# Last stage of a two-layer transformer kernel: PE issue order changed, last normalise as one scaled pass on ACT, last residual sum on DVE

## The chip, the cores and the metric

The kernel runs on one core of a Trainium2 chip. A core has five engines that run apart and meet through semaphores: TensorE (PE, matmuls), VectorE (DVE), ScalarE (ACT), GpSimd (POOL) and SyncE (SP), which here only issues DMAs. The metric is the device time of one execution in microseconds, and lower is better.

## The reference, cut to what matters

1024 tokens of width 512 pass through four sublayers, and after each one the sum of its input and its output is normalised. The change touches the last sublayer and the two normalisations around it:

```python
def _layernorm(x, axis=-1, eps=1e-05):
    m = jnp.mean(x, axis=axis, keepdims=True)
    v = jnp.var(x, axis=axis, keepdims=True)
    return (x - m) / jnp.sqrt(v + eps)

    dots = jax.nn.softmax(x @ centroids.T / TEMPERATURE, axis=-1)
    hits = dots > THRESHOLD
    query_sel = jnp.any(hits, axis=1)
    cluster_sel = jnp.any(hits, axis=0)
    row_sel = cluster_sel[assignments]
    dense = x @ weight.T + bias
    out = jnp.where(query_sel[:, None] & row_sel[None, :], dense, jnp.zeros((), dense.dtype))

x = _layernorm(x + _L0_attn_ref(...), axis=-1)
x = _layernorm(x + _L0_ffn_ref(...), axis=-1)
x = _layernorm(x + _L1_attn_ref(...), axis=-1)
x = _layernorm(x + _L1_ffn_ref(...), axis=-1)
```

`cluster_sel` needs the hits of all 1024 tokens, so no output row can be finished before the softmax over the 64 clusters is done for every token. The centroid matrix has 64 clusters.

## The kernel before, in words

Each sublayer is a stage of its own. The change lies in `gqa_stage`, after its loop over the eight key heads, where the last head is finished and the last sublayer is computed. The order of the work on every engine there is written out by hand: each engine's block lists its instructions, and semaphores hold one back until another has finished. Nothing is reordered by a scheduler. The tokens are eight tiles of 128 (`TT` = 8, `ST` = 4, so four tiles make one half, `b` = 0 or 1). Every fp32 product is made of three terms, high by high, low by high and high by low, so a merge, a logits step and a dense tile have 12 matmuls of 512 columns in groups of four, and a dense tile has two more for the bias.

The helpers that the prediction speaks of are these.

- On PE, `merge(True, tk, j)` adds the attention output of tile j in PSUM (line 1840), `turn_x(t)` transposes the normalised tile t into `ps_s` (line 1922), `logits(b)` multiplies one half by the centroids (line 1930), `turn_logits(b)` transposes the logits (line 1939), and `dense_tile(t, begin, end)` does the matmuls begin to end of 14 of dense tile t (line 1953). Between them two small steps count the hits (line 1988) and spread the chosen columns over the partitions (line 1992).
- On DVE, `sum_out(t)` adds a merge to X and takes mean and variance (lines 1687, 1681, 1683), `norm(t, base)` takes the reciprocal of the deviation and normalises X (lines 1694, 1696), and `low_x(t)` makes the low part of the turned tile (line 1701). `shift_logits` and `take_hits` are the softmax and the hits of one half (lines 1715 to 1730). The last loop over t does one masking pass of a dense tile out of PSUM (line 1764), then mean and variance of tile t-1 (`finish`) and the normalise of tile t-2.
- On ACT, `root(t, base)` is the square root of the variance (line 1555), `high_x(t)` the high part of the turned tile (line 1559), `take_logits(b)` copies the logits out of PSUM and `exp_soft(b)` is the exponential.
- On POOL, the last loop adds each masked dense tile to X (line 1495), and earlier one pass over the 512x512 weight makes its low part (line 1492).
- On SP, eight DMAs of 256 KB write the output tiles, each once its tile is normalised (line 1384).

Three facts set the order around the change. `turn_x(t)` waits for `norm(t)`, and from t = 2 for `low_x(t-2)`, since two PSUM banks take turns. `logits(0)` waits for `low_x(3)`. DVE runs `low_x(t-2)` between the statistics and the normalise of tile t, and ACT runs `root(t)` before `high_x(t-2)`.

Of the kernel before, what the change touches and what calls it, by code (L numbers as in the profile page):

```python
# [8 lines left out]
ACT = mybir.ActivationFunctionType  # L9
ALU = mybir.AluOpType  # L10
AXX = mybir.AxisListType.X

P = 128
# [5 lines left out]
TT = T // P  # L19
ST = S // P  # L20
# [1171 lines left out]
def gqa_stage(nc, ctx, dram, sb, mem, out):  # L1192
# [4 lines left out]
    with own:  # L1197
        def buf(name, shape, dt=F32):
            return own.enter_context(nc.sbuf_tensor(name, shape, dt))
# [4 lines left out]
        def sem(name):  # L1204
            return ctx.enter_context(nc.semaphore("gqa_" + name))

        X, xh, xl, ident = sb["X"], sb["xh"], sb["xl"], sb["ident"]
# [35 lines left out]
        bias = tables[0:1, 0, :]  # L1243
# [14 lines left out]
        any_hit = buf("any_hit", [P, NB, NCL])  # L1258
        moments = buf("moments", [P, TT, 2])
        dev = buf("dev", [P, TT])  # L1260
        eps = buf("eps", [P, 1])
        unused = buf("unused", [P, 1])
        KV, LAST = NKV - 1, NU * (NKV - 1) + NU - 1
# [51 lines left out]
        dense_added = sem("dense_added")  # L1315
        dense_counted = sem("dense_counted")
        stored = sem("stored")
        gate_sp, gate_pool = sb["gate_sp"], sb["gate_pool"]


# [67 lines left out]
        def _(pool):  # L1388
# [101 lines left out]
            pool.wait_ge(cl_step, 4)  # L1490
            pool.wait_ge(w_high, 1)
            pool.tensor_tensor(wl, w_raw, wh, ALU.subtract).then_inc(cl_ready, 1)
            for t in range(TT):
                pool.wait_ge(dense_taken, t + 1)
                pool.tensor_tensor(X[:, t, :], X[:, t, :], dense[:, t % 2, :], ALU.add).then_inc(dense_added, 1)

        @block.scalar
        def _(act):
            def values(kv, b):
                act.wait_ge(made, START + PER * kv + b + 1)  # L1500
                act.activation(probsT[:, b, :], ps_r[(START + b) % 2][:, :], ACT.Copy).then_inc(v_taken, 1)

            def turned_values(kv, b):
                act.wait_ge(v_turned, NB * kv + b + 1)
                act.activation(V[:, b, :, :], ps_t[b][:, :].rearrange("p (t n) -> p t n", t=ST), ACT.Copy)\
                   .then_inc(v_ready, 1)

            def softmax(i, u):
                for k, t in enumerate((3, 2, 0, 1)):

                    act.wait_ge(maxed, ST * i + (3 if k == 1 else k + 1))
                    bank, at = place[t]
                    n = (t + 1) * P
                    act.activation(probs[:, u % 2, t, 0:n], ps_s[bank][:, at:at + n], ACT.Exp,  # L1514
                                   bias=minus_max[:, t:t + 1], accum_out=sums[:, u % 2, t:t + 1]).then_inc(exped, 1)

            def take_turned(kv, u, k):

                act.wait_ge(turned, 3 * (NU * kv + u) + k + 1)
                n = S if k < 2 else 2 * P  # L1520
                act.activation(probsT[:, k, 0:n], ps_t[(u + k) % 2][:, 0:n], ACT.Copy).then_inc(t_taken, 1)  # L1521

            def take_outputs(kv, u):

                i = NU * kv + u
                act.wait_ge(pv_made, i + 1)
                act.activation(O[0][:, u % 2, u // 2, :], ps_o[:, :], ACT.Copy).then_inc(o_high, 1)  # L1527

            act.sem_inc(exped, ONE)
            act.wait_ge(wqkv_in, 32)  # L1530
            for parts, raw, _ in first_splits:
                act.activation(parts[0], raw, ACT.Copy).then_inc(step, 1)
            def body(kv, last):
                i = NU * kv
                softmax(i, 0)
                values(kv, 0)
                values(kv, 1)
                turned_values(kv, 0)
                turned_values(kv, 1)
                for u in range(1, NU):  # L1540
                    take_turned(kv, u - 1, 0)
                    take_turned(kv, u - 1, 1)
                    softmax(i + u, u)
                    take_turned(kv, u - 1, 2)
                    take_outputs(kv, u - 1)
                for k in range(3):
                    take_turned(kv, NU - 1, k)
                if not last:
                    take_outputs(kv, NU - 1)

            run(act, body)

            def root(t, base):
                act.wait_ge(mean_var, base + t + 1)
                act.activation(dev[:, t:t + 1], moments[:, t, 1:2], ACT.Sqrt, bias=eps[:, 0:1]).then_inc(rooted, 1)

            def high_x(t):
                act.wait_ge(x_turned, x_base + t + 1)
                act.activation(xh[:, :, t * P:(t + 1) * P], x_banks[t % 2][:, :].rearrange("p (c n) -> p c n", c=DC),
                               ACT.Copy).then_inc(x_high, 1)  # L1560

            def take_logits(b):
                act.wait_ge(logits_made, b + 1)
                act.activation(logits_T[:, b, :], (ps_c, ps_h)[b][0:NCL, :], ACT.Copy).then_inc(logits_taken, 1)

            def exp_soft(b):
                rows = soft[:, b * ST:(b + 1) * ST, :]
                act.wait_ge(shifted, b + 1)
                act.activation(rows, rows, ACT.Exp, scale=1.0 / TEMPERATURE).then_inc(soft_exped, 1)

            act.wait_ge(w_in, 16)
            act.wait_ge(made, ROPED)
            act.activation(wh, w_raw, ACT.Copy).then_inc(w_high, 1)
            act.wait_ge(eps_set, 3)
            act.activation(unused[:, :], eps[:, :], ACT.Sqrt)
            root(0, x_base)
            take_outputs(KV, NU - 1)
            root(1, x_base)
            for t in range(2, TT):
                root(t, x_base)  # L1580
                high_x(t - 2)
                if t == TT - 2:
                    take_logits(0)
            act.activation(unused[:, :], eps[:, :], ACT.Exp)
            high_x(TT - 2)
            high_x(TT - 1)
            exp_soft(0)
            take_logits(1)
            exp_soft(1)
            act.activation(unused[:, :], eps[:, :], ACT.Sqrt)  # L1590
            for t in range(TT):
                root(t, x_base + TT)

        @block.vector
        def _(dve):
# [95 lines left out]
            def norm(t, base):  # L1691
# [4 lines left out]
                dve.tensor_scalar(X[:, t, :], X[:, t, :], moments[:, t, 0:1], dev[:, t:t + 1],  # L1696
                                  ALU.subtract, ALU.mult).then_inc(x_normed, 1)

            def low_x(t):
                dve.wait_ge(x_high, x_base + t + 1)  # L1700
                dve.tensor_tensor(xl[:, :, t * P:(t + 1) * P], x_banks[t % 2][:, :].rearrange("p (c n) -> p c n", c=DC),
                                  xh[:, :, t * P:(t + 1) * P], ALU.subtract).then_inc(x_low, 1)
# [57 lines left out]
            for t in range(TT):  # L1760
                dve.wait_ge(dense_made, t + 1)
                if t >= 2:
                    dve.wait_ge(dense_added, t - 1)
                dve.scalar_tensor_tensor(out=dense[:, t % 2, :], in0=d_banks[t % ND][:, :], scalar=hit[:, t:t + 1],  # L1764
                                         in1=column, op0=ALU.mult, op1=ALU.mult).then_inc(dense_taken, 1)
                if t:
                    finish(t - 1)
                if t >= 2:
                    norm(t - 2, x_base + TT)
            finish(TT - 1)  # L1770
            norm(TT - 2, x_base + TT)
            norm(TT - 1, x_base + TT)

        @block.tensor
        def _(pe):
# [185 lines left out]
            merge(True, tk, 1)  # L1961
            outputs(LAST, NU - 1)
            merge(True, tk, 2)
            for t in range(TT - 3):
                turn_x(t)
                if t == 0:
                    merge(True, tk, 3)
                    pe.wait_ge(o_low, ONE + LAST + 1)
                    continue
                if t == ST:  # L1970
                    pe.wait_ge(cl_ready, 1)
                    logits(0)
                merge(True, tk, t + 3)
            turn_x(TT - 3)
            turn_logits(0)
            turn_x(TT - 2)
            pe.wait_ge(cl_ready, 3)
            dense_tile(0)
            turn_x(TT - 1)
            dense_tile(1)  # L1980
            logits(1)
            dense_tile(2, 0, 6)
            turn_logits(1)
            dense_tile(2, 6)
            dense_tile(3)
            for b in range(NB):
                pe.wait_ge(hits, b + 1)
                last = pe.matmul(ps_c[0:NCL, 0:1], any_hit[:, b, :], ones[:, 0:1], start=b == 0, stop=b == NB - 1)
            last.then_inc(hits_counted, 1)
            dense_tile(4, 0, 6)  # L1990
            pe.wait_ge(onehot_made, 1)
            pe.matmul(ps_h[:, :], ones[0:NCL, :], onehot, start=True, stop=True).then_inc(column_made, 1)
            dense_tile(4, 6)
            for t in range(5, TT):
                dense_tile(t)


# [106 lines left out]
```

## Time and profile before

| what | value |
|---|---|
| median of three runs | 2517.71 us |
| the three runs | 2509.70, 2517.71, 2518.99 us |
| the profiled execution's own time | 2519.56 us |
| its span, first to last instruction | 2517.5 us |
| mean granted TensorE clock | 0.99 of full |
| PE busy | 2465.6 us, 98% |
| DVE, ACT, POOL busy | 1555.6, 1396.0, 1152.8 us |
| the stretch that the change touches | 2448 to 2517.5 us |

All times in the rows count from the span's start. A busy PE is not a PE at its peak: matmuls are pipelined, and neighbouring ones overlap in the rows. So the distance from one start to the next tells what a step takes of the PE, and the duration of a row tells a little more. Square brackets at a row's end tell how long the engine stood idle just before, and which engine's instruction ended it.

### The profile page before, as it was taken

What the parts mean: (1) busy time and instruction counts of PE and PEld (TensorE: products, weight loads), DVE (VectorE), ACT (ScalarE), POOL (GpSimd) and SP (SyncE); (2) the same over time, 40 slices, a digit from 0 to 9 for tenths busy, and PEclk for the clock granted to TensorE, in tenths of its full rate; (3) what the DMA queues carried; (4) which work ended last, traced back from release to release, by engine and by line L of the source; (5) the groups of instructions that cost most, each with busy time, mean ns of one, the idle gap of its engine ahead of it and who ended that gap; (6) DMA issues with size and microseconds to landing.
All of it is one profiled execution on the core that took longest, in us unless ns stands there. A gap on an engine that the chain in (4) does not pass through costs nothing. (4 is left out here: it accounts for less than half of the span.)

```text
span 2517.5 us, 40557 instructions
## 1 busy us (share of the span) xinstructions
PE 2465.6 (98%) x12632; PEld 1858.7 (74%) x12632; DVE 1555.6 (62%) x2796; ACT 1396.0 (55%) x2171; POOL 1152.8 (46%) x1155
## 2 busy tenths in 40 slices
PE   7999999999999999999998999899999999999998
PEld 4777777777777777777775588778888888888875
DVE  6666666666666666666664523276657557566576
ACT  3677777777777777777776433233424324234241
POOL 1556555555555555656564243234334234343331
PEclk9999999999999999999999999989999999999999
DMA  6122222222222222222221422121000010010100
GB/s 215 43 47 53 45 53 50 48 53 45 53 45 56 48 55 45 53 45 53 45 55 39 131 88 85 39 84 42 10 32 17 25 42 17 25 42 2 36 1 34
DMA packets 47613, 125.40 MB, mean 50 GB/s; under 512 B 6034, under 2 KB 23442, under 8 KB 41427
## 3 DMA queue, kind: packets, MB, share of 16 engines
q1 hardware_dynamic: 47570, 124.85, 18.5%
q8 instruction: 25, 0.41, 0.1%
q14 instruction: 18, 0.14, 0.0%
HBM read 80.27 MB, written 10.49 MB: 36 GB/s over the span
## 5 line engine op out<-in xcount | busy, mean ns | idle before, releaser
L427 DVE TENSOR_REDUCE row_max<-ps_max 128x1 f32<-128x512 f32 x1024 | 670.9, 688 | 193.0 <-PE ps_max L517 170.6
L292 POOL TENSOR_TENSOR p_parts<-probs,p_parts 128x1024 f16<-128x1024 f32 x256 | 547.5, 2149 | 367.0 <-ACT p_parts L346 366.0
L341 ACT ACTIVATE probs<-ps_score 128x1024 f32<-128x1024 f32 x512 | 523.1, 1022 | 241.8 <-PE ps_score L533 221.1
L531 PE MATMUL ps_score<-Q,K 128*128 128x512 f32 x1024 | 408.0, 398 | 2.2 <-ACT probs L341 2.1
L533 PE MATMUL ps_score<-Q,K 97*128 97x512 f32 x1024 | 407.1, 398 | 0.0
L517 PE MATMUL ps_max<-KX,Q 68*128 68x512 f32 x1024 | 378.8, 411 | 3.8 <-DVE row_max L427 3.6
L421 DVE TENSOR_TENSOR Q<-ps_x,Q 64x512 fp32r<-64x512 f32 x254 | 175.0, 689 | 241.9 <-ACT Q L336 238.2
L346 ACT ACTIVATE p_parts<-probs 128x1024 f16<-128x1024 f32 x256 | 269.5, 1053 | 4.0
L517 PEld LDWEIGHTS ps_max<-KX,Q 68*128 68x128 f32 x1024 | 189.3, 190 | 76.4 <-issue 28.1
L531 PEld LDWEIGHTS ps_score<-Q,K 128*128 128x128 f32 x1024 | 194.5, 190 | 60.4 <-ACT probs L341 12.0
L533 PEld LDWEIGHTS ps_score<-Q,K 97*128 97x128 f32 x1024 | 195.5, 191 | 39.3
L1422 POOL CAST q_hi<-roped 128x512 fp32r<-128x512 f32 x64 | 39.1, 611 | 404.6 <-DVE roped L1610 212.7
L1514 ACT ACTIVATE probs<-ps_s,minus_max 128x512 f32<-128x512 f32 (+3 forms) x256 | 131.7, 540 | 139.3 <-DVE minus_max L1617 139.3
L336 ACT ACTIVATE Q<-ps_x 64x512 fp32r<-64x512 f32 x254 | 150.6, 593 | 74.5 <-PE ps_x L502 73.0
L1521 ACT ACTIVATE probsT<-ps_t 128x512 f32<-128x512 f32 (+1 forms) x192 | 94.1, 525 | 157.2 <-PE ps_t L1819 156.8
L1829 PE MATMUL ps_o<-probsT,v 128*128 128x512 f32 (+3 forms) x512 | 149.2, 434 | 1.3 <-ACT probsT L1521 1.3
L502 PE MATMUL ps_x<-xl,w_hi 128*128 128x512 f32 x508 | 143.1, 404 | 0.0
L502 PE MATMUL ps_x<-xh,w_hi 128*128 128x512 f32 x508 | 140.2, 398 | 0.0
L502 PE MATMUL ps_x<-xh,w_lo 128*128 128x512 f32 x508 | 138.8, 396 | 0.0
L1527 ACT ACTIVATE o_hi<-ps_o 128x512 fp32r<-128x512 f32 x64 | 38.3, 599 | 170.7 <-PE ps_o L1829 170.7
L544 PE MATMUL ps_o<-probs,V_slot 128*32 128x512 f32 x1024 | 126.3, 612 | 3.4 <-ACT probs L341 3.4
L1829 PEld LDWEIGHTS ps_o<-probsT,v 128*128 128x128 f32 x512 | 83.1, 191 | 49.8 <-issue 30.1
(292 smaller groups left out, 4399.8 us busy)
## 6 DMA issues: line engine op xcount, KB each, us to landing
Q<-Q SPq DMA_DIRECT2D x64, 512.0 KB, 4.3
ffn_raw<-in_w_ffn SPq DMA_DIRECT2D x22, 768.0 KB, 4.4
w_raw<-in_w_qrope SPq DMA_DIRECT2D x32, 512.0 KB, 3.7
wq_raw<-in_wq SPq DMA_DIRECT2D x8, 1024.0 KB, 5.5
wo_raw<-in_wo SPq DMA_DIRECT2D x8, 1024.0 KB, 4.8
content_k<-probs SPq DMA_DIRECT2D x8, 512.0 KB, 6.8
Q<-content_q SPq DMA_DIRECT2D x64, 64.0 KB
K<-content_k SPq DMA_DIRECT2D x64, 64.0 KB
```

The lines of the kernel that those rows point to most:

```text
L292: pool.tensor_tensor(p_lo[:, j, :, :], probs[:, j, 0:PAIRED, :], p_hi[:, j, :, :], ALU.subtract)\
L336: ins = act.activation(Q2[0:ROPE, b, 2 * pair + k, :], src[k * ROPE:(k + 1) * ROPE, :], ACT.Copy)
L341: act.activation(probs[:, j, 2 * half:2 * half + 2, :], ps_score[half][:, :, :], ACT.Exp, scale=SCALE).then_inc(exped, 1)
L346: act.activation(p_hi[:, j, :, :], probs[:, j, 0:PAIRED, :], ACT.Copy).then_inc(p_high, 1)
L421: ins = dve.tensor_tensor(Q1[ROPE:P, b, 2 * pair + k, :], src[k * ROPE:(k + 1) * ROPE, :], Q2[0:ROPE, b, 2 * pair + k, :], ALU.subtract)
L427: dve.tensor_reduce(row_max[:, t, j:j + 1], ps_max[t % 2][:, :], axis=AXX, op=ALU.max)\
L502: last = pe.matmul(out[:, :], w[:, c, pair, :], sb[x][:, c, b * S:(b + 1) * S], start=third == c == 0, stop=third == 2 and c == DC - 1)
L517: pe.matmul(ps_max[t % 2][:, :], Q2[0:KC0, b, j, t * P:(t + 1) * P], KX[0:KC0, b, j, :], start=True, stop=True).then_inc(max_made, 1)
L531: pe.matmul(ps_score[half][:, k, :], K1[:, b, t * P:(t + 1) * P], Q1[:, b, j, :], start=True, stop=False)
L533: last = pe.matmul(ps_score[half][:, k, :], K2[0:MROW + 1, b, j, t * P:(t + 1) * P], Q2[0:MROW + 1, b, j, :], start=False, stop=True)
L1514: act.activation(probs[:, u % 2, t, 0:n], ps_s[bank][:, at:at + n], ACT.Exp, bias=minus_max[:, t:t + 1], accum_out=sums[:, u % 2, t:t + 1] ...
L1829: last = pe.matmul(ps_o[:, tile * P:S], V[:, b, tile, :], probsT[:, k, at:at + S - tile * P], start=tile == 0, stop=k == 2)
```

## The change

There are three edits.

1. PE, after the last head: `merge` of tile 7 stands ahead of `logits(0)`, the turns of tiles 6 and 7 stand ahead of the first dense tile, and the hits, the second logits and the chosen columns stand between earlier parts of the dense tiles. Dense tiles 0 and 1 and nine matmuls of tile 2 stand ahead of the chosen columns, where it was tiles 0 to 3 and six of tile 4. ACT's queue has `high_x(t-2)` ahead of `root(t)` now, and the first `take_logits` behind the load of the exponential's table.
2. The last normalise: DVE's pass over the tile becomes a product of 128x1, `shift` = -mean / deviation (`scale_out`), and ACT computes X / deviation + shift in one pass of 128x512 (`normal`).
3. The last residual sum: tile 7 of eight is added on DVE and not on POOL.

On PE, from the turn of tile 4 on, before. `ps_s<-ident,X` is `turn_x`, `ps_t<-...wkv` is `logits(0)`, and `ps_r<-wo` is the merge of tile 7:

```order
L1922 MATMUL ps_s<-ident,X 128x128 x4
L1930 MATMUL ps_t<-xh,wkv_hi 64x512 x4
L1930 MATMUL ps_t<-xl,wkv_hi 64x512 x4
L1930 MATMUL ps_t<-xh,wkv_lo 64x512 x4
L1840 MATMUL ps_r<-wo_hi,o_hi 128x512 x4
L1840 MATMUL ps_r<-wo_hi,o_lo 128x512 x4
L1840 MATMUL ps_r<-wo_lo,o_hi 128x512 x4
L1922 MATMUL ps_s<-ident,X 128x128 x4
L1939 MATMUL ps_s<-ident,probs 128x64 x4
```

The same place now, again from the turn of tile 4, to the transposes of the logits (`ps_s<-ident,probs`):

```order
L1945 MATMUL ps_s<-ident,X 128x128 x4
L1863 MATMUL ps_r<-wo_hi,o_hi 128x512 x4
L1863 MATMUL ps_r<-wo_hi,o_lo 128x512 x4
L1863 MATMUL ps_r<-wo_lo,o_hi 128x512 x4
L1945 MATMUL ps_s<-ident,X 128x128 x4
L1953 MATMUL ps_t<-xh,wkv_hi 64x512 x4
L1953 MATMUL ps_t<-xl,wkv_hi 64x512 x4
L1953 MATMUL ps_t<-xh,wkv_lo 64x512 x4
L1945 MATMUL ps_s<-ident,X 128x128 x8
L1976 MATMUL ps_o<-k_hi,ones_r 128x512 x2
L1976 MATMUL ps_o<-wq_hi,xh 128x512 x4
L1962 MATMUL ps_s<-ident,probs 128x64 x4
```

The merge of tile 7 and one turn have moved ahead of `logits(0)`, the last two turns follow it, and six dense matmuls stand between them and the transposes of the logits.

The end of DVE's queue, from the masking pass of tile 7 on, before:

```order
L1764 SCALAR_TENSOR_TENSOR probs<-ps_r,hit,probs 128x512
L1681 BN_STATS stats<-X 128x6
L1683 BN_AGGR moments<-stats 128x2
L1694 RECIPROCAL dev<-dev 128x1
L1696 TENSOR_SCALAR X<-X,moments,dev 128x512
L1681 BN_STATS stats<-X 128x6
L1683 BN_AGGR moments<-stats 128x2
L1694 RECIPROCAL dev<-dev 128x1
L1696 TENSOR_SCALAR X<-X,moments,dev 128x512
L1694 RECIPROCAL dev<-dev 128x1
L1696 TENSOR_SCALAR X<-X,moments,dev 128x512
```

The same place now:

```order
L1783 SCALAR_TENSOR_TENSOR probs<-ps_r,hit,probs 128x512
L1692 BN_STATS stats<-X 128x6
L1694 BN_AGGR moments<-stats 128x2
L1713 RECIPROCAL dev<-dev 128x1
L1715 TENSOR_SCALAR shift<-moments,dev 128x1
L1713 RECIPROCAL dev<-dev 128x1
L1715 TENSOR_SCALAR shift<-moments,dev 128x1
L1792 TENSOR_TENSOR X<-X,probs 128x512
L1692 BN_STATS stats<-X 128x6
L1694 BN_AGGR moments<-stats 128x2
L1713 RECIPROCAL dev<-dev 128x1
L1715 TENSOR_SCALAR shift<-moments,dev 128x1
```

Three passes of 128x512 have left DVE for ACT here, and one, the sum of tile 7, has come from POOL.

The core of the diff:

```diff
-            for t in range(TT):
+            for t in range(TT - 1):
                 pool.wait_ge(dense_taken, t + 1)
                 pool.tensor_tensor(X[:, t, :], X[:, t, :], dense[:, t % 2, :], ALU.add).then_inc(dense_added, 1)
...
+            def normal(t):
+                act.wait_ge(shift_set, t + 1)
+                act.activation(X[:, t, :], X[:, t, :], ACT.Identity, scale=dev[:, t:t + 1],
+                               bias=shift[:, t:t + 1]).then_inc(x_normed, 1)
...
             for t in range(2, TT):
+                high_x(t - 2)
                 root(t, x_base)
-                high_x(t - 2)
-                if t == TT - 2:
-                    take_logits(0)
             act.activation(unused[:, :], eps[:, :], ACT.Exp)
+            take_logits(0)
             high_x(TT - 2)
...
             for t in range(TT):
+                if t == TT - 1:
+                    normal(t - 1)
                 root(t, x_base + TT)
+                if 0 < t < TT - 1:
+                    normal(t - 1)
+            normal(TT - 1)
...
+            def scale_out(t):
+                at = TT + root_base + t + 1
+                dve.wait_ge(rooted, at)
+                dve.reciprocal(dev[:, t:t + 1], dev[:, t:t + 1]).then_inc(inverse_set, 1)
+                dve.wait_ge(inverse_set, at)
+                dve.tensor_scalar(shift[:, t:t + 1], moments[:, t, 0:1], dev[:, t:t + 1], -1.0,
+                                  ALU.mult, ALU.mult).then_inc(shift_set, 1)
...
                 if t >= 2:
-                    norm(t - 2, x_base + TT)
+                    scale_out(t - 2)
+            scale_out(TT - 2)
+            dve.wait_ge(dense_taken, TT)
+            dve.wait_ge(dense_added, TT - 1)
+            dve.tensor_tensor(X[:, TT - 1, :], X[:, TT - 1, :], dense[:, (TT - 1) % 2, :], ALU.add)\
+               .then_inc(dense_added, 1)
             finish(TT - 1)
-            norm(TT - 2, x_base + TT)
-            norm(TT - 1, x_base + TT)
+            scale_out(TT - 1)
...
-            turn_x(TT - 3)
+            turn_x(ST + 1)
+            pe.wait_ge(cl_ready, 1)
+            logits(0)
+            turn_x(TT - 2)
+            turn_x(TT - 1)
+            pe.wait_ge(cl_ready, 3)
+            dense_tile(0, 0, 6)
             turn_logits(0)
-            turn_x(TT - 2)
-            pe.wait_ge(cl_ready, 3)
-            dense_tile(0)
-            turn_x(TT - 1)
-            dense_tile(1)
+            dense_tile(0, 6)
             logits(1)
-            dense_tile(2, 0, 6)
+            dense_tile(1, 0, 4)
             turn_logits(1)
-            dense_tile(2, 6)
-            dense_tile(3)
+            dense_tile(1, 4)
+            dense_tile(2, 0, 4)
...
-            dense_tile(4, 0, 6)
+            dense_tile(2, 4, 9)
             pe.wait_ge(onehot_made, 1)
             pe.matmul(ps_h[:, :], ones[0:NCL, :], onehot, start=True, stop=True).then_inc(column_made, 1)
-            dense_tile(4, 6)
-            for t in range(5, TT):
+            dense_tile(2, 9)
+            for t in range(3, TT):
                 dense_tile(t)
```

## Rows read from the trace of the kernel before

**Rows 1.** Windows: span, busy PE, PEld, DVE, ACT, POOL, then clock, DMA share, GB/s.

```profile
2462.00:2470.00 8.00, 5.49 (x19) 3.23 (x20) 5.49 (x12) 1.86 (x5) 0.00 (x0) 0.79 0.00 0
2470.00:2496.00 26.00, 26.00 (x114) 17.30 (x113) 11.65 (x27) 6.55 (x12) 0.00 (x0) 1.00 0.00 1
```

**Rows 2.** Timeline of PE, turns of tiles to `logits(0)`: start, duration, what.

```profile
2451.66 0.60 PE L1922 MATMUL ps_s<-ident,X 128*128 128x128 f32 x4
...
2454.87 0.60 PE L1922 MATMUL ps_s<-ident,X 128*128 128x128 f32 x4
...
2461.97 0.66 PE L1922 MATMUL ps_s<-ident,X 128*128 128x128 f32 x4
2465.14 1.74 PE L1930 MATMUL ps_t<-xh,wkv_hi 128*64 128x512 f32 x4 [2.51 <-DVE xl L1701]
...
2469.49 1.09 PE L1840 MATMUL ps_r<-wo_hi,o_hi 128*128 128x512 f32 x4
```

**Rows 3.** Timeline of DVE and ACT, one period of the tile loop.

```profile
2456.84 0.69 DVE L1701 TENSOR_TENSOR xl<-ps_s,xh 128x512 fp32r<-128x512 f32 x1 [0.85 <-ACT xh L1559]
...
2459.76 0.29 ACT L1555 ACTIVATE dev<-moments,eps 128x1 f32<-128x1 f32 x1 [2.96 <-DVE moments L1683]
...
2460.57 0.69 DVE L1701 TENSOR_TENSOR xl<-ps_s,xh 128x512 fp32r<-128x512 f32 x1 [0.84 <-ACT xh L1559]
```

**Rows 4.** Timeline of PE, `logits(1)` to dense tile 7.

```profile
2481.41 1.09 PE L1930 MATMUL ps_t<-xh,wkv_hi 128*64 128x512 f32 x4
...
2484.26 0.73 PE L1953 MATMUL ps_r<-k_hi,ones_r 1*128 1x512 f32 x2
...
2486.05 0.46 PE L1939 MATMUL ps_s<-ident,probs 64*128 64x64 f32 x4
...
2488.50 0.72 PE L1953 MATMUL ps_s<-k_hi,ones_r 1*128 1x512 f32 x2
...
2492.15 0.39 PE L1988 MATMUL ps_t<-ones_sb,any_hit 128*64 128x1 f32 x4
...
2494.25 1.12 PE L1992 MATMUL ps_t<-probs,ones_sb 64*128 64x512 f32 x2
...
2504.67 0.73 PE L1953 MATMUL ps_r<-k_hi,ones_r 1*128 1x512 f32 x2
```

**Rows 5.** Timeline of DVE, softmax of half 1 to the last normalise.

```profile
2486.62 0.42 DVE L1715 TENSOR_REDUCE top<-ps_s 128x4 f32<-128x256 f32 x1 [3.67 <-PE ps_s L1939]
...
2489.44 0.61 DVE L1728 TENSOR_REDUCE any_hit<-probs 128x64 f32<-128x256 f32 x1
...
2492.66 0.15 DVE L1753 TENSOR_SCALAR chosen<-ps_t 64x1 f32<-64x1 f32 x1 [2.27 <-PE ps_t L1988]
...
2495.41 0.69 DVE L1759 COPY probs<-ps_t 128x512 f32<-128x512 f32 x1 [2.04 <-PE ps_t L1992]
2496.14 0.75 DVE L1764 SCALAR_TENSOR_TENSOR probs<-ps_o,hit,probs 128x512 f32<-128x512 f32 x1
...
2510.61 0.74 DVE L1764 SCALAR_TENSOR_TENSOR probs<-ps_r,hit,probs 128x512 f32<-128x512 f32 x1
...
2514.53 0.55 DVE L1696 TENSOR_SCALAR X<-X,moments,dev 128x512 f32<-128x512 f32 x1
```

**Rows 6.** Groups of instructions by form: busy us, mean ns of one, idle before.

```profile
L1681 DVE BATCH_NORM_STATS2 stats<-X 128x6 f32<-128x512 f32 x16 | 11.0, 688 | 1.0 <-POOL X L1495 0.7
...
L972 ACT ACTIVATE ffn_w_hi<-ffn_raw 128x512 fp32r<-128x512 f32 x22 | 13.6, 617 | 0.0
...
L1590 ACT ACTIVATE unused<-eps 128x1 f32<-128x1 f32 x1 | 0.2, 203 | 0.0
```

**Rows 7.** Timelines of DVE and of POOL around 2443 us.

```profile
2443.22 4.72 DVE L1696 TENSOR_SCALAR X<-X,moments,dev 128x512 f32<-128x512 f32 x1
...
2443.09 4.57 POOL L1492 TENSOR_TENSOR wq_lo<-wq_raw,wq_hi 128x2048 fp32r<-128x2048 f32 x1
```

**Rows 8.** DMA issues of 2436 to 2518 us: KB each, median us to landing.

```profile
out<-X SPq DMA_DIRECT2D x8, 256.0 KB, 2.0
```

More of the change, by code:

```diff
@@ L1260, in gqa_stage @@
         dev = buf("dev", [P, TT])
+        shift = buf("shift", [P, TT])
         eps = buf("eps", [P, 1])
@@ L1317, in gqa_stage @@
         stored = sem("stored")
+        shift_set = sem("shift_set")
         gate_sp, gate_pool = sb["gate_sp"], sb["gate_pool"]
@@ L1963, in _ @@
             merge(True, tk, 2)
-            for t in range(TT - 3):
+            for t in range(ST + 1):
                 turn_x(t)
+                merge(True, tk, t + 3)
                 if t == 0:
-                    merge(True, tk, 3)
                     pe.wait_ge(o_low, ONE + LAST + 1)
[L1969 to L1973, printed above, removed]
-            turn_x(TT - 3)
-            turn_logits(0)
-            turn_x(TT - 2)
-            pe.wait_ge(cl_ready, 3)
-            dense_tile(0)
-            turn_x(TT - 1)
-            dense_tile(1)
+            turn_x(ST + 1)
[5 more added lines that the diff above has]
+            dense_tile(0, 0, 6)
+            turn_logits(0)
+            dense_tile(0, 6)
             logits(1)
-            dense_tile(2, 0, 6)
+            dense_tile(1, 0, 4)
             turn_logits(1)
-            dense_tile(2, 6)
-            dense_tile(3)
+            dense_tile(1, 4)
+            dense_tile(2, 0, 4)
             for b in range(NB):
```

## The prediction, made before the changed kernel was run

> **What bounds the kernel now.** I read the busy shares first: PE is busy 98% of the span, so what is left to win is where PE stands still or runs slowly, and what runs behind its last matmul. The chain of waits, followed back from the end, shows the two places. From 2496 to 2515 us it runs through DVE alone, tile after tile; before that, from 2465 to 2496 us, it is PE without a gap; and from 2441 to 2465 us it alternates between DVE and ACT. Then I read the timelines.
>
> The first place is the tile loop. Each period of DVE takes 3.73 us (2456.84 to 2460.57) and holds a wait of 0.84 us for ACT's high part, which stands behind the square root in ACT's queue [rows 3]. PE alone needs 3.21 us per tile for a merge and a turn (2451.66 to 2454.87) [rows 2]. So DVE leads the loop and PE falls behind its own pace: the turn of tile 4 starts at 2461.97. Then PE waits 2.51 us for `low_x(3)`, and `logits(0)` takes 4.35 us, from 2465.14 to 2469.49 [rows 2], where `logits(1)`, with the same 12 matmuls, takes 2.85 us (2481.41 to 2484.26) [rows 4]. The granted clock is 0.79 in the 8 us around it and 1.00 in the 26 us behind [rows 1]. That is the upper level, 2.4 GHz, behind, and a mixture with 1.2 GHz around the wait.
>
> The second place is the end. Dense tile 7 starts on PE at 2504.67 [rows 4]. A dense tile takes 3.65 us: 1.79 for its first six matmuls (2484.26 to 2486.05), and 2.45 for the transposes of the logits and the last eight (2486.05 to 2488.50), of which I put 0.39 on the transposes, as the hits' four small matmuls take [rows 4], and 2.06 on the eight. That is 3.85, and 0.2 less where a tile runs in one piece. So the last dense tile is there at about 2508.4, but DVE takes it at 2510.61, 2.2 us later [rows 5]. DVE is the bound at the end, by 2.2 us. From that start to the end of the last normalise are 4.47 us (2514.53 + 0.55), and 2.42 more to the end of the span, for a DMA that lands 2.0 us after its issue [rows 8].
>
> **Part 1, the order on PE and ACT.** The ACT order first. With `high_x(t-2)` ahead of `root(t)` the high part is ready when DVE asks, and the square root (0.29 us) runs beside `low_x` (0.69 us) [rows 3]. The period of DVE falls by about 0.84 plus a small overlap, to 2.8 or 2.9 us. That is below PE's 3.21, so PE now sets the pace: counted on from its turn of tile 1 at 2451.66, the turn of tile 4 starts three periods later, at 2461.27 and not 2461.97. This gives 0.7 us. It needs `norm(4)` by then. `low_x(1)` starts at 2456.84 now, so `low_x(0)` a period earlier at 2453.1, and without its wait at 2452.3. Two new periods on, `low_x(2)` starts near 2458.0, and `norm(4)` ends about 1.35 behind that start (0.69, then 0.15 and 0.55 by the tiny and the 128x512 rows of [rows 5]), at 2459.3. PE doesn't wait there.
>
> Next comes the wait. `low_x(3)` is now ready near 2461.5, and `logits(0)` stands behind merge 7 and the turn of tile 5, at about 2464.8. The wait of 2.51 us and about 0.3 us of draining and restarting around it go. With no wait ahead of it I take `logits(0)` at 2.85 us, which gives 1.50. The turn of tile 7 needs `norm(7)`. Its sum waits for merge 7, which ends near 2464.6 (2461.27 + 3.21 and a little drain); a period of 2.9 us later `norm(7)` is ready, at 2467.5. PE ends `logits(0)` at 2467.65 and gets to that turn, the second of two, at 2468.0. The margin is 0.5 us, the smallest before the hits.
>
> So from the turn of tile 4 to the start of dense tile 7 the same instructions took 42.70 us (2461.97 to 2504.67). Less 2.82 and 1.50 that is 38.38, and dense tile 7 starts at 2461.27 + 38.38 = 2499.65: 5.0 us earlier.
>
> What stands in the way are the hits. The two turns take about 0.95 together, so the first dense tile starts near 2468.6; 1.79, the transposes 0.39, 2.06, `logits(1)` 2.85 and four dense matmuls (1.2) bring the second transposes to 2476.9. Their maximum starts 0.57 later, and from it to the end of `any_hit` are 3.43 us (2486.62 to 2490.05) [rows 4, 5], so the hits are made at 2480.9. PE gets there at 2476.9 + 0.39 + 2.6 + 1.2 = 2481.1. That is a margin of 0.2 us. The chosen columns are made by DVE about 1.25 us after the hits' matmul starts, at 2482.35 (0.51 to `chosen` [rows 4, 5], then a pass that I estimate at 0.6 from a row of 0.42 for 256 elements), and PE arrives at 2481.1 + 0.39 + 1.3 = 2482.8. The margin is 0.4 us. The column is copied 1.16 us after its matmul starts, and the first masking pass follows 0.73 behind [rows 4, 5]: near 2484.6, where it was 2496.14.
>
> **What DVE then does.** Before, DVE took 14.47 us from the masking pass of tile 0 to that of tile 7 (2496.14 to 2510.61) [rows 5]. Even at that old pace it would be at tile 7 at 2499.1, and the tile itself comes at 2499.65 + 3.72 = 2503.4. So DVE waits for PE in the end, the 2.2 us vanish, and taking the normalise off DVE in the loop is worth nothing by itself. What edits 2 and 3 are worth is what they do behind the last masking pass.
>
> **Parts 2 and 3, the end.** Counted from the start of the masking pass of tile 7 at 2503.4: the pass 0.7, the statistics of tile 6 0.7 [rows 6] and their second step 0.2, the square root 0.3 [rows 3], reciprocal and `shift` of tile 6 0.3 (a DVE instruction on 64x1 takes 0.15 [rows 5]). That makes 2.2. Then the sum of tile 7 on DVE, 0.7 as in `low_x` [rows 3], statistics 0.9, square root 0.3, reciprocal and `shift` 0.3, and some 0.05 in handoffs: 4.45. Then ACT's pass. No row has it in this form. A pass of 128x512 from SBUF takes 0.617 with no operand of one value per partition [rows 6]; one such operand costs 0.09, by the square root with one (0.29 [rows 3]) against the table warm-up without (0.20 [rows 6]). With two it is 0.80. The bounds are 0.62 and 1.0. I take 0.80, which gives 5.25 against 4.47. So the end is 0.8 us longer. ACT's other passes are in time: `normal(6)` ends about 0.5 us before the last square root is asked for.
>
> The new DVE instruction `shift` and the seven sums that stay on POOL could meet. The normalise of tile 0, normally 0.55 us long, took 4.72 us while POOL's pass of 4.57 us ran [rows 7]. The Trainium skill, "SBUF — State Buffer", "Who interferes with whom", says that VectorE in a two-port mode and GpSimd take a shared port pair as a lock for a whole instruction; these rows agree. Were `shift` held like that, it would last until POOL's sum ends (a quarter of the 4.57, so about 1.2 us long), up to 0.5 us more per tile, in a loop with 1 us or more to spare, so neither the sum nor a chance changes.
>
> **The sum.** 5.0 (PE) + 2.2 (DVE's lag) - 0.8 (the longer end) = 6.4 us. The profiled execution took 2519.56, so it would take 2513.2; that execution stood 1.9 above the median, which gives 2517.71 - 6.4 = 2511.3. I say 2511.
>
> **The rivals.**
> - *A wait comes back at the hits.* The margins are 0.2 and 0.4 us, so a small error makes PE wait. For: they are the smallest in the new order. Against: a wait of 0.5 us costs 0.5. Only a long one, of some 2.5 us, brought the low clock, with 1.5 us more. Bounds of the loss are 0.3 and 4.0; I take 2. The time is 2513.
> - *The end alone, no faster PE.* If `logits(0)` stays slow and the turn of tile 7 is late, only the lag of 2.2 and the 2.5 us wait count, less 0.8: about 4 us, 2514.
> - *Slower: the dense stage runs at the low clock.* All eight turns and both transposes of logits are short matmuls, and three turns now stand close together. At low clock a matmul of 512 costs about 0.39 us (1.74 for four that overlap) against 0.26 in a dense tile [rows 2, 4]. The gain of 6.4 is used up after 49 matmuls, three and a half of the eight dense tiles; if all 112 were slow it would cost 15 us, net 8 slower: 2526. Against: before, two turns and the transposes of logits stood in a row between 2470 and 2474, and the clock was 1.00 from 2470 to 2496 [rows 1]. The Trainium skill, "TensorE: Matmul & The Clock Gate", "Part 4: PE-mode transpose", says that transposes do not count as work for the clock as other matmuls do. By that rule this rival would bite; the trace shows no such fall.
>
> **Chances.** The forecast 0.68, the wait at the hits 0.15, the end alone 0.08, slower by the clock 0.04, and 0.05 for what I don't see on either side. What a measurement of this kernel can tell from no change is about 0.5%, 12.6 us. My forecast, 6.4 us or 0.25%, lies within, and so do all the rivals but part of the slow one. The four times known of before spread over 9.9 us (2509.7 to 2519.56), so a median of a few runs can stray by 3 or 4 us beyond what the work does. That takes the range to 2504 and 2518, and gives faster by over 0.5% 0.08, within 0.5% 0.89, slower by over 0.5% 0.03.
>
> **What would show it.** `logits(0)` starts near 2464.8 with no wait ahead of it and takes 2.85 us; DVE's waits for the high part are gone; dense tile 7 starts near 2499.7; the masking pass of tile 7 waits for PE, as do those from tile 4 on; the last ACT pass takes 0.8 us and ends near 2508.6; the span is 2511. Wrong would be a wait over 1 us at lines 2008 or 2012, a granted clock below 1.00 between 2462 and 2500, or a table load between the last passes of ACT.

## The result, and the profile after

The changed kernel takes 2508.78 us (median of 22 runs, 2504.72 to 2516.03) where the kernel before takes 2515.12 (22 runs, 2509.62 to 2521.75). The ratio is 0.9977, with a 95% interval of 0.9969 to 0.9985. By the ratio that is 5.8 us less, with 3.8 to 7.8 in the interval; the two medians lie 6.3 us apart. It is a small gain, clear of noise, and within the 0.5% that I had called no change. The forecast was 6.4 us less and a time of 2511.

The two profiles differ by more, 2517.5 against 2502.5 us of span, and most of that lies ahead of the change. To keep the two apart I count the tail from here on: from the start of the turn of tile 0, right behind the merge of tile 2, to the end of the span. Up to there no engine has an instruction more or less. The turn of tile 0 starts at 2448.47 before and at 2439.42 after, so 9.05 us of the difference lie ahead of it. The tail is 69.03 us before and 63.08 us after: 5.95 us less.

These are windows of the profile after (span, busy PE, PEld, DVE, ACT, POOL, clock, DMA share, GB/s). They answer to [rows 1]:

```profile
2448.00:2456.00 8.00, 8.00 (x43) 6.62 (x42) 7.62 (x18) 2.08 (x5) 0.00 (x0) 1.00 0.00 0
2456.00:2462.00 6.00, 6.00 (x32) 3.85 (x30) 3.83 (x9) 3.82 (x7) 0.00 (x0) 1.00 0.02 4
2462.00:2484.00 22.00, 22.00 (x88) 13.60 (x87) 13.46 (x34) 5.43 (x10) 5.08 (x4) 1.00 0.03 13
```

The clock is 1.00 from the tile loop through the dense tiles, where 0.79 stood around the logits. PE's timeline after, against [rows 2] and [rows 4], the hits included:

```profile
2439.42 0.60 PE L1945 MATMUL ps_s<-ident,X 128*128 128x128 f32 x4
...
2452.22 0.60 PE L1945 MATMUL ps_s<-ident,X 128*128 128x128 f32 x4
...
2455.76 1.16 PE L1953 MATMUL ps_t<-xh,wkv_hi 128*64 128x512 f32 x4
...
2458.58 1.03 PE L1945 MATMUL ps_s<-ident,X 128*128 128x128 f32 x8
...
2472.11 0.39 PE L2008 MATMUL ps_t<-ones_sb,any_hit 128*64 128x1 f32 x4
...
2490.82 0.73 PE L1976 MATMUL ps_r<-k_hi,ones_r 1*128 1x512 f32 x2
```

The turn of tile 4 starts 12.80 us behind that of tile 0, where it was 13.50. The logits follow without a wait in brackets and take 2.82 us (2455.76 to 2458.58). The last dense tile starts 51.40 us behind the turn of tile 0, where it was 56.20.

DVE's timeline after, against [rows 3] and [rows 5]: two neighbouring tiles of the loop, then the end.

```profile
2448.66 0.66 DVE L1720 TENSOR_TENSOR xl<-ps_s,xh 128x512 fp32r<-128x512 f32 x1
...
2451.43 0.66 DVE L1720 TENSOR_TENSOR xl<-ps_s,xh 128x512 fp32r<-128x512 f32 x1
...
2471.25 0.60 DVE L1747 TENSOR_REDUCE any_hit<-probs 128x64 f32<-128x256 f32 x1
...
2475.68 0.75 DVE L1783 SCALAR_TENSOR_TENSOR probs<-ps_o,hit,probs 128x512 f32<-128x512 f32 x1
...
2494.58 0.75 DVE L1783 SCALAR_TENSOR_TENSOR probs<-ps_r,hit,probs 128x512 f32<-128x512 f32 x1 [1.78 <-PE ps_r L1976]
...
2496.84 0.68 DVE L1792 TENSOR_TENSOR X<-X,probs 128x512 f32<-128x512 f32 x1
2497.56 0.69 DVE L1692 BATCH_NORM_STATS2 stats<-X 128x6 f32<-128x512 f32 x1
...
2499.03 0.21 DVE L1715 TENSOR_SCALAR shift<-moments,dev 128x1 f32<-128x1 f32 x1
```

And ACT's last pass, the new form that no row of before had:

```profile
2499.27 0.81 ACT L1561 ACTIVATE X<-X,shift,dev 128x512 f32<-128x512 f32 x1 [0.48 <-DVE shift L1715]
```

The period of the loop is 2.77 us and its wait for ACT is gone. The last masking pass waits 1.78 us for PE, so PE and not DVE is the bound at the end. Behind that pass's start the normalised tile is ready after 5.50 us (2494.58 to 2500.08), where it was 4.47.

### The profile page after: what moved, and what is told of

It reads as the page before. It is cut to its first block and busy times, and to the rows that moved or that the text cites. A ratio compares the mean times of both kernels' runs of the same rounds, so it can differ in the third digit from the quotient of the medians.

```text
span 2502.5 us, 40566 instructions
## 1 busy us (share of the span) xinstructions
PE 2455.2 (98%) x12632; PEld 1851.7 (74%) x12632; DVE 1551.4 (62%) x2797; ACT 1403.4 (56%) x2179; POOL 1151.9 (46%) x1154
```

## The experiments

All of them are judged by the tail of their profile, and each is one profiled execution; only the kernel with the last tile on DVE was also timed over several runs. The tail can be compared from run to run, as the whole span can't. Two profiles of the changed kernel agree in it within 0.02 us. Where PE waits so long that the low clock follows, it varies too: by 1.2 us in the two profiles of before.

| kernel | tail, us | expected |
|---|---|---|
| before, two profiles | 69.03, 70.26 | |
| all three edits, two profiles | 63.08, 63.10 | 63.08 |
| order alone | 62.08 | 62.05 |
| edits 2 and 3 alone | 69.10 | 67.9 |
| all edits, ACT's order as before | 69.64 | 68.2 to 69.7 |
| before, ACT's order swapped | 64.03 | 64.1 |
| all edits, PE's order as before | 62.93 | 63.0 |
| all edits, sum of tile 7 on POOL | 62.49 | 62.4 |
| hits four matmuls earlier | 63.90 | 63.9 to 64.1 |
| tile 6 ahead of the last masking pass | 61.73 | 61.55 |
| the same, last tile normalised on DVE | 61.23 | 61.1 |
| the same, PE's order as before | 62.39 | 62.3 |

**Order alone.** The kernel before with PE's and ACT's new order only; the later place of the first `take_logits` belongs to it.

> Edit 1 alone (the order on PE and on ACT), with the normalise on DVE and all eight sums on POOL as before. I count the tail, from the start of the turn of tile 0 (right behind the merge of tile 2) to the end of the span: 69.03 us before, 63.08 us with all three edits. My theory: DVE waits for PE in the last tiles even at its old pace, so edits 2 and 3 only lengthen the end behind the last masking pass (5.50 against 4.47 us). Order alone then gives 63.08 - 1.03 = 62.05 us. Rival: DVE's shorter loop is needed to use the faster PE; then the tail is 65 us or more, and the last masking pass does not wait for PE.

Measured: span 2510.7, the turn of tile 0 at 2448.62, so 62.08 us, 1.0 less than with all three edits. DVE's timeline has the last masking pass waiting for PE, although every period still holds the whole normalise:

```profile
2503.78 0.75 DVE L1763 SCALAR_TENSOR_TENSOR probs<-ps_r,hit,probs 128x512 f32<-128x512 f32 x1 [1.24 <-PE ps_r L1952]
...
2507.71 0.55 DVE L1695 TENSOR_SCALAR X<-X,moments,dev 128x512 f32<-128x512 f32 x1
```

The end is 4.48 us again (2503.78 to 2508.26). On top of the new order, edits 2 and 3 cost 1.0 us. The rival falls.

**Edits 2 and 3 alone.** The kernel before with the scaled pass on ACT and the sum of tile 7 on DVE.

> Edits 2 and 3 alone, with PE's and ACT's order as before. My theory: PE keeps its wait of 2.5 us and its slow logits, the last dense tile comes as before; DVE's shorter loop (1.77 us per tile) takes away its lag of 2.2 us and the longer end costs 1.0, so the tail is 69.03 - 1.1 = 67.9 us. Rival: most of the gain of 5.95 us comes from the lighter DVE loop: the tail is 64 to 65 us.

Measured: 2512.9 - 2443.80 = 69.10 us. Both theories miss it. The last masking pass waits 0.39 us for PE, as I expected, and the end is 5.50 us; but PE itself is 1.2 us later than in the profile of before. Its timeline shows where. It has the same wait, but a longer stretch of slow matmuls behind it:

```profile
2460.50 1.94 PE L1954 MATMUL ps_t<-xh,wkv_hi 128*64 128x512 f32 x4 [2.51 <-DVE xl L1721]
2462.24 1.91 PE L1954 MATMUL ps_t<-xl,wkv_hi 128*64 128x512 f32 x4
2463.95 1.91 PE L1954 MATMUL ps_t<-xh,wkv_lo 128*64 128x512 f32 x4
2465.65 1.47 PE L1864 MATMUL ps_r<-wo_hi,o_hi 128*128 128x512 f32 x4
```

The logits take 5.15 us, not 4.35. That called for the next one.

**The kernel before again.**

> The kernel before, unchanged, for a second profile. The kernel with edits 2 and 3 alone had the same wait of 2.51 us ahead of the logits, but its low clock lasted 6 us and not 4, so the logits took 5.15 us and not 4.35 and more of the merge behind them was slow. My theory: how long the low clock lasts behind that wait differs from one execution to the next, so this tail is 69.0 to 70.3 us, with the logits at 4.3 to 5.2 us. Rival: the length belongs to the kernel; the logits take 4.35 us again and the tail is 69.0 within 0.1.

Measured: 2518.3 - 2448.04 = 70.26 us. PE's timeline:

```profile
2464.73 1.94 PE L1930 MATMUL ps_t<-xh,wkv_hi 128*64 128x512 f32 x4 [2.52 <-DVE xl L1701]
2466.47 1.91 PE L1930 MATMUL ps_t<-xl,wkv_hi 128*64 128x512 f32 x4
2468.17 1.91 PE L1930 MATMUL ps_t<-xh,wkv_lo 128*64 128x512 f32 x4
2469.88 1.47 PE L1840 MATMUL ps_r<-wo_hi,o_hi 128*128 128x512 f32 x4
```

And its windows there, at the lower level, 1.2 GHz, for all of the logits:

```profile
2465.00:2470.00 5.00, 5.00 (x13) 2.72 (x12) 3.02 (x7) 0.78 (x2) 0.00 (x0) 0.50 0.00 0
2470.00:2472.00 2.00, 2.00 (x9) 1.61 (x8) 0.00 (x0) 0.59 (x1) 0.00 (x0) 0.82 0.00 0
```

The same kernel with the same wait loses 1.2 us more here than in its first profile. So the tail of before is 69.0 or 70.3 us, and what the change wins differs with it: 5.95 or 7.2 us. Against the longer one, edits 2 and 3 alone win 70.26 - 69.10 = 1.16, which is the 1.1 that I had expected. That is a fair pair: the last dense tile starts 57.4 us behind the turn of tile 0 in both.

**The changed kernel again.**

> The changed kernel, unchanged, for a second profile. My theory: its PE never waits behind the turn of tile 0, so nothing in its tail can differ: 63.08 us within 0.1, whatever the rest of the span does. Rival: the tail differs as much as the whole span does, by several us.

Measured: 2504.4 - 2441.30 = 63.10 us, the first within 0.02.

**ACT's order taken back.** All edits, with `root(t)` ahead of `high_x(t-2)` again.

> All three edits, but ACT takes the square root ahead of the high part in the tile loop, as before. My theory: this order on ACT is what makes PE wait. DVE's period stays 3.73 us, PE waits for the turn of tile 7 for some 3 us and the first dense tile starts 5 us later, and the clock drops for another 1.5: the tail is 68.2 to 69.7 us. Rival: PE's own order (merge 7 ahead of the logits) is what counts: the tail stays within 1 us of 63.1.

Measured: 2512.8 - 2443.16 = 69.64 us. PE's timeline shows the wait and the slow matmuls behind it, now in dense tile 0:

```profile
2467.85 0.66 PE L1945 MATMUL ps_s<-ident,X 128*128 128x128 f32 x4 [3.08 <-DVE X L1707]
2468.44 0.73 PE L1976 MATMUL ps_o<-k_hi,ones_r 1*128 1x512 f32 x2
2469.09 1.95 PE L1976 MATMUL ps_o<-wq_hi,xh 128*128 128x512 f32 x4
```

DVE's period is 3.73 us again. The tail lies between the two profiles of before, so without the swap on ACT the rest of the change wins nothing that can be told from their spread.

**ACT's order alone.** Two lines of the kernel before change places:

```diff
             for t in range(2, TT):
-                root(t, x_base)
                 high_x(t - 2)
+                root(t, x_base)
```

> The kernel before with one change: in ACT's tile loop the high part stands ahead of the square root. My theory: this takes PE's wait of 2.5 us and the slow logits away even with PE's old order (the turn of tile 4 starts 12.8 us behind that of tile 0, and no wait follows), so the last dense tile comes 4.8 to 5.0 us earlier; DVE still has its lag, since the chosen columns come late and its loop takes 14.47 us: the tail is 64.1 us. Rival: without PE's new order the wait stays, and the tail is 67 us or more.

Measured: 2511.9 - 2447.87 = 64.03 us. No wait of PE is left in the tail, and the last dense tile starts 51.19 us behind the turn of tile 0, 0.2 earlier than in the changed kernel. The last masking pass waits for nobody, 14.47 us behind the first: DVE has its lag still. This swap is worth 5.0 of the 5.95 us, or 6.2 of 7.2 against the second profile of before. That it does so through DVE's period and PE's wait is shown by the two runs together: the period is 2.77 us with the swap and 3.73 without it.

**PE's order taken back.** All edits but PE's; the first `take_logits` goes back to its old place too, and no run moves it alone.

> All three edits, but PE's instructions in the order before; ACT has the high part ahead of the square root. My theory: PE never waits here either, the chosen columns come at the old place, some 4.9 us earlier than before, and DVE's shorter loop (11.8 us from its first to its last masking pass) ends about when the last dense tile comes. The tail is 63.0 us, so PE's new order is worth nothing once ACT's order and DVE's loop are changed. Rival: PE's new order is worth 1 us or more: 64 us and up.

Measured: 2509.8 - 2446.87 = 62.93 us, 0.15 better than the changed kernel. The last masking pass waits 0.39 us for PE. So PE's new order and DVE's lighter loop remove the same lag of 2.2 us. Counted from the turn of tile 0, that pass starts at 57.13 with ACT's order alone, at 55.16 with PE's order added, at 54.95 with edits 2 and 3 added, and at 55.16 with both. In the tail edits 2 and 3 win only 1.1 us (64.03 to 62.93), since they lengthen the end by 1.0; PE's order wins 1.95 (64.03 to 62.08).

**The sum of tile 7 on POOL.** The changed kernel without edit 3.

> All three edits but the third: the sum of tile 7 goes back to POOL. My theory: POOL's sum of 1.28 us runs beside DVE's work on tile 6 and ends 2.1 us behind the start of the last masking pass; DVE is ready for the statistics of tile 7 at 2.3, where it starts them at 2.98 now. The tail is 63.08 - 0.65 = 62.4 us. Rival, the reason for the edit: POOL's pass is twice as long as DVE's, so its return costs 0.6 us: 63.7.

Measured: 2505.2 - 2442.71 = 62.49 us. POOL's pass is longer, 1.26 us, but it runs beside DVE's work on tile 6. On DVE the sum stands in the line that sets the end.

**Hits four matmuls earlier.**

```diff
             dense_tile(1, 4)
-            dense_tile(2, 0, 4)
...
-            dense_tile(2, 4, 9)
+            dense_tile(2, 0, 9)
```

> All three edits, and the four matmuls of dense tile 2 that stand ahead of the hits' matmul stand behind it. The hits are made 0.26 us before PE asks for them now, so PE should wait 0.8 to 1.0 us here. My theory: a wait of that length costs itself and leaves the granted clock at the upper level: the tail is 63.9 to 64.1 us. Rival: the wait brings the low clock, as the one of 2.5 us did in the kernel before: 1.5 us more, 65.5 us.

Measured: 2507.2 - 2443.30 = 63.90 us, with the wait in PE's timeline, and then the windows around it, with the clock as the third number from the end:

```profile
2475.77 0.28 PE L2007 MATMUL ps_t<-ones_sb,any_hit 128*64 128x1 f32 x2 [0.83 <-DVE any_hit L1747]
```

```profile
2473.00:2476.00 3.00, 2.17 (x13) 1.47 (x11) 2.38 (x7) 1.90 (x3) 0.00 (x0) 1.00 0.01 3
2476.00:2478.00 2.00, 2.00 (x9) 1.41 (x9) 0.73 (x3) 0.00 (x0) 0.00 (x0) 1.00 0.00 0
```

A wait of 0.83 us cost 0.82 us, and the granted clock stayed at 1.00.

**Tile 6 ahead of the last masking pass.**

```diff
             for t in range(TT):
+                if t == TT - 1:
+                    finish(t - 1)
+                    scale_out(t - 2)
+                    scale_out(t - 1)
                 dve.wait_ge(dense_made, t + 1)
...
-                if t:
+                if 0 < t < TT - 1:
                     finish(t - 1)
-                if t >= 2:
+                if 2 <= t < TT - 1:
                     scale_out(t - 2)
-            scale_out(TT - 2)
```

> All three edits, and DVE does the statistics and the scale of tile 6 (and the scale of tile 5) ahead of the last masking pass and not behind it, while it waits for PE. My theory: this wait of 1.78 us hides that work, and the end behind the start of the last masking pass falls from 5.50 to 3.97 us: the tail is 61.55 us. Rival: the statistics wait for POOL's sum of tile 6 and push the masking pass of tile 7 back, so that less than 0.7 us are won.

Measured: 2509.3 - 2447.57 = 61.73 us. The masking pass starts about 0.1 us late, since the statistics wait 0.29 us for POOL's sum of tile 6; 1.35 us are won.

**The last tile on DVE too.** As above, and `norm(TT - 1, x_base + TT)` in place of the last `scale_out` and `normal`.

> As the kernel with tile 6 ahead of the last masking pass, and the last tile alone is normalised on DVE in one pass and not by scale on DVE and pass on ACT. My theory: 0.55 us of DVE replace shift (0.2), the handoff and ACT's pass of 0.81, so the end is 3.5 us and the tail 61.1 us; in time that is 8 us under the kernel before, a ratio of 0.9968. Rival: the pass on DVE is as long as ACT's, or the output DMA sets the end: no more than 0.2 us against the kernel without it.

Measured: 2506.9 - 2445.67 = 61.23 us. DVE's timeline of the end:

```profile
2500.94 0.74 DVE L1786 SCALAR_TENSOR_TENSOR probs<-ps_r,hit,probs 128x512 f32<-128x512 f32 x1
2501.72 0.69 DVE L1794 TENSOR_TENSOR X<-X,probs 128x512 f32<-128x512 f32 x1
2502.45 0.69 DVE L1691 BATCH_NORM_STATS2 stats<-X 128x6 f32<-128x512 f32 x1
...
2503.92 0.55 DVE L1706 TENSOR_SCALAR X<-X,moments,dev 128x512 f32<-128x512 f32 x1
```

The end is 3.53 us. In time it is 2506.68 us (8 runs) against 2514.19 (13 runs of before), a ratio of 0.9963, with 0.9949 to 0.9977. It is faster than the kernel before by a little, clear of noise. Against the changed kernel its tail is 1.85 us shorter, but the two were not timed side by side and their intervals overlap.

**The same with PE's order as before.**

> The kernel with tile 6 ahead of the last masking pass and the last tile normalised on DVE, but with PE's instructions in the order before. With all three edits alone the old PE order gave a tail of 62.93 us against 63.08, because DVE caught up 0.4 us before the last dense tile came. My theory: PE's new order is worth something only where DVE needs that time, and here it does: the work on tile 6, 1.6 us, stands ahead of the last masking pass, which then starts about 1.2 us late. The tail is 62.3 us, against 61.23 with PE's new order. Rival: the two PE orders are the same everywhere, and the tail is 61.1 to 61.3 us.

Measured: 2504.9 - 2442.51 = 62.39 us. Here PE's new order is worth 1.16 us, because DVE needs the time that it gives.

## Why the prediction was right

The steps held in kind, and the sum of 6.4 us stands against 5.95 in the tails of the first two profiles (4.80 from PE, 2.18 from DVE's lag, less 1.03 at the end) and 5.8 in the timed runs. That the time came out at 2508.78 and not at 2511 comes from the base: the median of three runs of before was 2517.71, that of 22 is 2515.12. Point by point, in distances from the turn of tile 0 (2448.47 before):

- *The tile loop.* Forecast: DVE's period 2.8 or 2.9 us, PE's pace 3.21, the turn of tile 4 at 12.80. Measured: 2.77, and 12.80. (Three periods of 3.21 from 2451.66 give 2461.29 and not 2461.27; nothing hangs on it.) The turn of tile 7 was to be met with a margin of 0.5 us, and PE waits nowhere.
- *The wait and the slow logits.* Forecast: both gone, the logits 2.85 us. Measured: gone, 2.82. The last dense tile was to start at 51.18 and starts at 51.40, 4.80 us earlier and not 5.0. The kernel with ACT's swap alone, which doesn't cut its early dense tiles so often, has 51.19. So the missing 0.2 lies in PE's new order, and both kernels have no wait here. From the turn of tile 0 to the last dense tile, and by distances from start to start, the dense matmuls take 26.27 us in the changed kernel and 25.77 with the swap alone, nearly all of it where their groups are cut into more pieces; the turns take 3.07 and 3.40. That fits the more frequent change between tiles as the cause.
- *The margin at the hits.* Forecast 0.2 us, measured 0.26 (`any_hit` ends at 2471.85, PE gets there at 2472.11). The run with earlier hits shows the rival's price at a wait of 0.83 us: the wait itself and no clock, where I had taken 2 us for this rival.
- *DVE's lag.* Forecast: 2.2 us gone, DVE waits for PE from tile 4 on. Measured so, with 1.78 us at the last tile; 1.24 at the old pace, in the kernel with the order alone.
- *The end.* Forecast 0.8 us longer; it is 1.03 (5.50 against 4.47), and this is the term that was mis-sized most, by 0.25 us. ACT's pass was right, 0.81 against 0.80 from the rows. The Trainium skill, "ScalarE: Activation LUTs", "What ACT_TABLE_LOAD costs", gives 186 ns, 0.833 ns per element and 93 ns for each pointer operand; by it I estimate the pass at 0.80, and the trace agrees with 0.81. Too low was `shift`, 0.21 us a piece where I took the 0.15 of a neighbour, and the handoffs between DVE and ACT.
- *`shift` and POOL.* It takes 0.21 us at 2499.03 with POOL idle, and the rows below of the changed kernel's timeline show the same 0.21 while POOL's sum runs. So it isn't held up there, other than the pass over 512 elements of [rows 7]. What I overlooked is that the old normalise was held in the last loop as well: the last two rows are of the kernel before. Six such passes beside a sum on POOL take 0.72 to 0.76 us, the two with POOL idle 0.55, and all six and the one of [rows 7] end 0.3 us behind POOL's instruction.

```profile
2484.45 1.29 POOL L1497 TENSOR_TENSOR X<-X,probs 128x512 f32<-128x512 f32 x1 [1.94 <-DVE probs L1783]
...
2485.27 0.21 DVE L1715 TENSOR_SCALAR shift<-moments,dev 128x1 f32<-128x1 f32 x1
```

```profile
2502.23 1.29 POOL L1495 TENSOR_TENSOR X<-X,probs 128x512 f32<-128x512 f32 x1 [1.02 <-DVE probs L1764]
...
2503.05 0.76 DVE L1696 TENSOR_SCALAR X<-X,moments,dev 128x512 f32<-128x512 f32 x1
```

- *Slower by the low clock.* It did not come: the clock is 1.00 through all eight turns and the dense tiles.

What I did not see is how uneven the base is. I took the 4.35 us of the slow logits as a fixed size. In the second profile of before they take 5.15, and the merge behind them is slow at first too; the tail is 1.2 us longer, so the same working would have given 7.6 us from there, where 7.2 are measured. That 6.4 comes so near rests in part on which execution was profiled.

## What to carry to other kernels

In a loop over two engines, look at what stands ahead of the instruction that the other engine waits for. Two lines in another order on ACT, an engine with much idle time, were worth 5.0 of 5.95 us, because they took a wait and a slow stretch from PE, the busiest engine. Once the bound has moved, ask of each remaining edit which wait it shortens: PE's new order and the lighter DVE loop removed the same lag, and moving the last sum to DVE and the last normalise to ACT, each idle at times there, lengthened the chain behind the last matmul by 1.0 us. What helps that chain is to put work that isn't on it into the wait ahead of it. And where the whole varies by several us, compare the profiles from a common point just ahead of the change.

## What the runs showed that I had not expected

The spread of the whole, 10 us or more in either kernel, lies mostly in the granted clock at places that the change doesn't touch. The clearest is the start. These are the windows from 60 to 70 us, of the kernel before:

```profile
60.00:70.00 10.00, 9.98 (x17) 4.98 (x16) 1.98 (x3) 3.64 (x6) 1.87 (x2) 0.50 0.13 42
```

of the changed kernel:

```profile
60.00:70.00 10.00, 9.49 (x38) 6.59 (x37) 5.50 (x9) 5.82 (x9) 5.62 (x5) 1.00 0.12 32
```

and of the kernel before in its second profile:

```profile
60.00:70.00 10.00, 9.99 (x13) 3.50 (x11) 0.40 (x1) 3.48 (x6) 1.88 (x2) 0.50 0.18 51
```

PE gets through 17 or 13 matmuls in these 10 us at the lower clock and through 38 at the higher. They aren't the same steps, so the counts give no rate, but a like pair does: eight matmuls into `ps_score` take 6.72 us from the first start to the next step in the first profile of before, and 3.63 in the changed kernel. The changed kernel is the one at the higher clock here, in both of its profiles over the first 100 us (mean 0.98). But the other kernels, whose code up to there is the same as its own, have 0.85 to 0.93 in that stretch. The start of the turn of tile 0 goes with it in all 14 profiles but one: it is at 2439.4 and 2441.3 us at 0.98, at 2442.5 to 2445.7 at 0.91 to 0.93, and at 2446.9 to 2448.6 at 0.85 and 0.86. The exception is the first profile of before, at 2448.47 with 0.91. It also has a clock of 0.90 from 1350 to 1400 us and 0.83 from 1620 to 1670, where three others at 0.91 have 0.97 and 0.90. So I take this for a difference between executions and not for a part of the change. Whether the changed code behind it makes the good case more likely stays open: two profiles can't tell.

Windows of half a us show how long the lower clock lasted behind PE's waits. Behind the wait of 2.51 us in the first profile of before it lasted 3.4 us, and behind that of 3.08 us 3.4 as well. With the same wait of 2.5 us it lasted 6.8 us in the second profile of before and in the kernel with edits 2 and 3 alone; there it began 0.9 us before the wait ended, and in the first profile of before 0.2 us after. Behind the wait of 0.83 us there was none.
